# A two-stage mixture-of-experts kernel: the hand-written order of work where its two stages meet is planned anew

## The reference, cut to what matters

```python
x = x + xattn(layernorm(x), token_ids, ctx)   # 4 experts, chosen by token id
x = x + ffn(layernorm(x), router_w, wg, wu, wd)  # 8 experts, chosen by argmax of the logits
# xattn, expert e:  y = (silu(h @ ctx[e].T) * (h @ ctx[e].T)) @ ctx[e].T
# ffn, expert e (bitlinear: weights to -1, 0, 1 times a mean; activations to int8 by row):
#   y = bitlinear(relu(bitlinear(h, wg[e]))**2 * bitlinear(h, wu[e]), wd[e])
```

## Time and profile before

| | |
|---|---|
| median of 3 runs | 247.35 us (246.73 to 247.69) |
| the profiled execution | 247.17 us |
| its span, first to last instruction | 245.3 us |
| mean granted TensorE clock | 0.989 |
| PE, DVE, ACT, POOL busy | 218.7, 209.0, 197.7, 160.4 us |

### The profile page before, as it was taken

The page is one execution under the profiler, slowest core; times in us unless marked ns, Lnnn a source line. Parts: engine busy times, 40 slices in busy tenths (PEclk is TensorE's granted clock), DMA queues, the critical chain, the costliest instruction groups (busy, mean ns, idle before and its releaser), DMA issues.

```text
span 245.3 us, 6263 instructions
## 1 busy us (share of the span) xinstructions
PE 218.7 (89%) x1622; PEld 170.4 (69%) x1629; DVE 209.0 (85%) x696; ACT 197.7 (81%) x297; POOL 160.4 (65%) x324
## 2 busy tenths in 40 slices
PE   2398999999999999999999999987789999899970
PEld 2245688889899999999999998976334544343430
DVE  5969999977969899899988999979799998888771
ACT  2757799877768889998999979896678998788860
POOL 5262667756637598888987887553734878557762
PEclk9999999999999999999999999999979999999998
DMA  5999999996985266679565786335328899994120
GB/s 199 426 319 383 413 421 385 402 378 187 392 302 174 81 263 218 254 261 339 166 245 212 251 252 220 95 122 178 97 50 241 289 293 366 379 387 190 65 108 13
DMA packets 14273, 61.44 MB, mean 250 GB/s; under 512 B 2654, under 2 KB 2654, under 8 KB 9632
## 3 DMA queue, kind: packets, MB, share of 16 engines
q1 hardware_dynamic: 9600, 47.60, 53.6%
q0 software_dynamic: 4640, 13.44, 15.6%
HBM read 43.88 MB, written 12.70 MB: 231 GB/s over the span
## 4 chain that ended last, share of the span: by engine, by line
PE 68%; DVE 14%; DMA 7%; issue 6%; ACT 3%; POOL 1%; DVEq 0%; ACTq 0%; POOLq 0%
PE banks L1834 35%; PE banks L2014 15%; PE banks L1817 7%; DMA ternary<-weight_chunks 4%; PE banks L2016 4%; DMA x<-x_rows,gather 2%; PE banks L2003 2%; PE banks L1979 2%; PE banks L1859 2%; POOL out_rows L778 1%; DVE stats L1249 1%; DVE row L1305 1%; PE banks L1887 1%; DVE ternary L1108 1%; DVE p L1285 1%
## 5 line engine op out<-in xcount | busy, mean ns | idle before, releaser
L833 ACT ACTIVATE ternary<-staged 128x2048 bf16<-128x2048 f32 x20 | 38.1, 1906 | 1.8 <-DMA staged<-weight_chunks 1.8
L2014 PE MATMUL banks<-ternary,qT 128*128 x126 | 34.6, 394 | 3.3 <-ACT qT L922 1.6
L839 ACT ACTIVATE ternary<-staged,w_scale 128x1536 int16<-128x1536 f32 (+1 forms) x20 | 34.4, 1724 | 2.9 <-DVE w_scale L1202 2.9
L692 POOL DMA_INDIRECT x_rows<-row,store_at x19 | 22.3, 1172 | 9.3 <-POOL store_at L684 6.9
L1834 PE MATMUL banks<-ctx_hi,pT_hi 128*128 x132 | 23.0, 313 | 1.7 <-DVE row L1305 1.1
L594 POOL DMA_INDIRECT x<-x_rows,gather x16 | 18.3, 1145 | 9.2 <-DVE gather L1120 6.3
L647 POOL TENSOR_TENSOR row<-ln,half_powers 128x2 f32<-128x2 f32 x19 | 14.1, 744 | 14.9 <-DVE squares L1320 14.9
L2014 PEld LDWEIGHTS banks<-ternary,qT 128*128 128x128 bf16 x128 | 12.4, 101 | 16.4 <-issue 8.5
L1834 PE MATMUL banks<-ctx_hi,hT_hi 128*128 x132 | 22.8, 312 | 0.0
L1834 PE MATMUL banks<-ctx_lo,hT_hi 128*128 x132 | 21.2, 300 | 0.2 <-DVE ctx_lo L1149 0.2
L1834 PE MATMUL banks<-ctx_hi,pT_lo 128*128 x132 | 21.3, 301 | 0.0
(11 more groups left out here) (284 smaller groups left out, 641.0 us busy)
## 6 DMA issues: line engine op xcount, KB each, us to landing
staged<-weight_chunks SPq DMA_DIRECT2D x20, 1024.0 KB
twin<-ternary SPq DMA_DIRECT2D x4, 1536.0 KB
ternary<-ctx_chunks SPq DMA_DIRECT2D x4, 1024.0 KB, 7.9
ternary<-weight_chunks SPq DMA_DIRECT2D x4, 1024.0 KB, 12.3
ternary<-ctx_rows SPq DMA_DIRECT2D x4, 1024.0 KB, 11.0
late_rows<-x_rows SPq DMA_DIRECT2D x11, 260.0 KB, 3.0
x_rows<-filler SPq DMA_DIRECT2D x1, 2080.0 KB
staged<-x_rows SPq DMA_DIRECT2D x5, 260.0 KB, 3.5
```

Of the source, the lines that this page charges most:

```text
L692: pool.indirect_dma_start(x1_rows, bass.IndirectOffsetOnAxis(ap=store_at[b % ROWS][:, :], axis=0), row[b % ROWS][:, :], None, bounds_check ...
L833: nc.scalar.activation(ternary[:, m * K * D:(m + 1) * K * D], staged_of(i), ACT.Abs, accum_out=abs_sum[:, 2 * i:2 * i + 1]).then_inc(abs_r ...
L839: nc.scalar.activation(ternary[:, m * K * D + first:(m + 1) * K * D].bitcast(I16), staged_of(i)[:, first:], ACT.Copy, scale=w_scale[:, m:m ...
L2014: last = pe.matmul(ps[:, :], rows, ternary[:, columns], start=(k == 0), stop=(k == K - 1))
```

## The change

- EARLY becomes 6 and EARLY_AFTER 15: six slots are planned from the counts of blocks 0 to 15, and 14 are left for later. GROUPS, LATE and the places follow.
- The last second product (block 18) writes the half banks 4 and 5, those of the first products, and waits for `kept_ready` in place of the residual of block 17. The gate products of stage 2 start in bank 3 instead of 4.
- The sum of matrix 20 moves into first_product(18), ahead of its third pass; that of matrix 21 stays ahead of the third pass of second_product(18), and its result goes to bank 7. transpose_q(0) goes to the same place.
- The loops of DVE, ACT and PE end a tick sooner (at t = 17), and the rest is written out in a new order; the nine steps of `early_slots` now begin at the end of tick 17 and are strewn over what follows.
- down_product(1) waits until `late_slots` has read the counts.

The diff, cut to its core (`next(early)` and `next(factors)` are one step each):

```diff
-EARLY, EARLY_AFTER = 5, 14
+EARLY, EARLY_AFTER = 6, 15
+        def second_banks(b):
+            return (4, 5) if b == B1 - 1 else (2, 3)
+        def mean_ps(i, n=1):
+            return bank[7][:, 300:300 + n] if i == len(ORDER) - 1 else bank[6][:, 64 + 2 * i:64 + 2 * i + n]
-        g_ps, u_ps = [bank[4], bank[3]], [bank[1], bank[2]]
+        g_ps, u_ps = [bank[3], bank[4]], [bank[1], bank[2]]
 # ACT, behind the loop
+            evict_pT(B1 - 2)
+            scale_piece(*EXTRA_SCALES[B1 - 1])
+            scale_part(B1 - 1 + ABOVE)
+            silu(B1 - 1)
+            square(B1 - 3)
             evict_pT(B1 - 1)
             sum_abs(B1 + ABOVE)
             square(B1 - 2)
+            evict_tT(0)
             scale_part(B1 + ABOVE)
-            evict_tT(0)
+            evict_tT(1)
             square(B1 - 1)
-            evict_tT(1)
             relu_of(0)
+            evict_tT(2)
             square_of(0)
-            evict_tT(2)
             relu_of(1)
+            evict_tT(3)
             square_of(1)
             copy_by_slot(0)
             quantise_prod(0)
-            evict_tT(3)
 # DVE, end of tick 17 and behind the loop
+                if t == B1 - 2:
+                    next(early)
+                if t > 2:
                     cut(t + ABOVE - 1)
+            next(early)
+            cut(B1 - 2 + ABOVE)
+            next(early)
+            sum_logits(B1 - 3)
+            residual(B1 - 3)
+            next(early)
+            top_logits(B1 - 3)
+            negative_mean(B1 - 3)
+            next(early)
+            choice(B1 - 3)
+            mean_of(B1 - 1 + ABOVE)
+            scale_of(B1 - 1 + ABOVE)
+            scale_part(B1 - 1 + ABOVE)
+            one_hot(B1 - 3)
+            pT_rest(B1 - 2)
+            extra_cut(EXTRA_CUT[B1])
+            next(early)
+            gate(B1 - 1)
+            keep_logits(B1 - 1)
+            next(early)
             cut(B1 - 1 + ABOVE)
+            row_index(B1 - 3)
+            next(early)
+            largest(B1 - 3)
+            next(early)
+            pT_rest(B1 - 1)
+            sum_logits(B1 - 2)
+            residual(B1 - 2)
+            negative_mean(B1 - 2)
+            quantise(0)
+            top_logits(B1 - 2)
+            choice(B1 - 2)
             mean_of(B1 + ABOVE)
             scale_of(B1 + ABOVE)
             scale_part(B1 + ABOVE)
+            one_hot(B1 - 2)
+            quantise(1)
             sum_logits(B1 - 1)
             residual(B1 - 1)
+            negative_mean(B1 - 1)
+            row_index(B1 - 2)
+            largest(B1 - 2)
             top_logits(B1 - 1)
             choice(B1 - 1)
+            quantise(2)
             one_hot(B1 - 1)
+            next(factors)
+            largest(B1 - 1)
+            next(factors)
             row_index(B1 - 1)
+            next(factors)
             product_of(0)
+            next(factors)
+            next(factors)
+            quantise(3)
             largest_product(0)
             cut(B1 + ABOVE)
             first_factors()
             product_scale(0)
-            quantise(3)
             late = late_slots()
 # PE
+        # first_product(18), ahead of pass n == 2: sum_mean(B1 - 1 + ABOVE)
+        # second_product(17), n == 1: rank(B1 - 3); n == 2: transpose_p(B1 - 1)
+        # second_product(18), n == 2: sum_mean(B1 + ABOVE), transpose_q(0)
+                if b == B1 - 1:
+                    pe.wait_ge(kept_ready, B1 - FOLD)
+            transpose_p(B1 - 2)
+            first_product(B1 - 1)
+            second_product(B1 - 2)
+            count_in(B1 - 3)
+            load_ffn_expert(0)
             second_product(B1 - 1)
-            transpose_q(0)
-            load_ffn_expert(0)
+            rank(B1 - 2)
             gate_product(0)
-            rank(B1 - 1)
             transpose_q(1)
             up_product(0)
             load_ffn_expert(1)
-            count_in(B1 - 1)
+            count_in(B1 - 2)
             gate_product(1)
+            rank(B1 - 1)
             transpose_q(2)
             up_product(1)
             load_ffn_expert(2)
+            count_in(B1 - 1)
             spread_means(0)
             gate_product(2)
             transpose_q(3)
```

More of the change, by code:

```diff
@@ L320, in y_of @@
         def y_of(b):
-            return y_ps if b < FOLD else banks[:, 2 * D + D // 2:3 * D + D // 2]
+            first = second_banks(b)[0] * D + D // 2
+            return y_ps if b < FOLD else banks[:, first:first + D]
         def chosen(t):
             return [b for b in (t - 3,) if b < FOLD] + [b for b in (t - 2,) if b >= FOLD]
-        counts_ps, mean_ps, logits_ps = bank[6][:, 0:E2], bank[6], bank[7]
+        counts_ps, logits_ps = bank[6][:, 0:E2], bank[7]
+        def mean_ps(i, n=1):
+            return bank[7][:, 300:300 + n] if i == len(ORDER) - 1 else bank[6][:, 64 + 2 * i:64 + 2 * i + n]
         tT_ps = bank[0][:, 0:D // 4].bitcast(BF16)
-        g_ps, u_ps = [bank[4], bank[3]], [bank[1], bank[2]]
+        g_ps, u_ps = [bank[3], bank[4]], [bank[1], bank[2]]
         rT_ps, d_ps = bank[7][:, 0:D // 4].bitcast(BF16), [bank[5], bank[6]]
@@ L990, in _ @@
             sum_abs(3)
-            for t in range(2, TICKS):
+            for t in range(2, B1 - 1):
                 evict_pT(t - 1)
@@ L1653, in _ @@
             early, factors = early_slots(), mean_products()
-            for t in range(2, TICKS):
-                interlude = early if t == EARLY_AFTER + 3 else iter(())
+            for t in range(2, B1 - 1):
                 first, *second = chosen(t)
@@ L1844, in columns_of @@
                 if second:
-                    return [(bank[2][:, half:], LEFT, half), (bank[3][:, 0:half + E2], LEFT + half, half + E2)]
+                    lower, upper = second_banks(b)
+                    return [(bank[lower][:, half:], LEFT, half), (bank[upper][:, 0:half + E2], LEFT + half, half + E2)]
                 return [(bank[4][:, half - E2:], 0, half + E2), (bank[5][:, 0:half], LEFT + half, half)]
@@ L1886, in sum_mean @@
                     pe.wait_ge(w_mean_ready, i)
-                pe.matmul(mean_ps[:, 64 + 2 * i:64 + 2 * i + n], ones[:, :], abs_sum[:, 2 * i:2 * i + n],
-                          start=False, stop=True, skip_group_check=True).then_inc(mean_ready, 1)
+                if i == len(ORDER) - 2:
+                    pe.wait_ge(counts_read, 1)
+                pe.matmul(mean_ps(i, n), ones[:, :], abs_sum[:, 2 * i:2 * i + n], start=(i == len(ORDER) - 1),
+                          stop=True, skip_group_check=True).then_inc(mean_ready, 1)
             def transpose_h(b):
@@ L1939, in ahead @@
                     def ahead(n):
+                        if n == 1:
+                            rank(B1 - 3)
                         if n == 2:
@@ L1946, in ahead @@
                     def ahead(n):
-                        if n == 1:
-                            rank(B1 - 2)
                         if n == 2:
-                            count_in(B1 - 2)
                             sum_mean(B1 + ABOVE)
+                            transpose_q(0)
                             pe.wait_ge(pT_lo_ready, B1)
-                if b >= 1:
+                if b == B1 - 1:
+                    pe.wait_ge(kept_ready, B1 - FOLD)
+                elif b >= 1:
                     pe.wait_ge(x1_ready, b)
@@ L2125, in down_product @@
                     pe.wait_ge(relu_ready, B2 - 1)
-                elif b > 1:
+                elif b == 1:
+                    pe.wait_ge(counts_read, 2)
+                else:
                     pe.wait_ge(out_ready, b - 1)
@@ L2154, in _ @@
             second_product(0)
-            for t in range(2, B1):
+            for t in range(2, B1 - 1):
                 transpose_p(t - 1)
```

56 lines of the change are left out of this document (15 added, 41 removed).

## The result

| | before | changed |
|---|---|---|
| median of 11 runs each, side by side | 246.89 us | 248.71 us |
| ratio, 95% interval | | 1.0068 (1.0047 to 1.0088) |
| profiled execution, its span | 247.17, 245.3 us | 248.56, 246.7 us |
| mean granted TensorE clock | 0.989 | 0.981 |
| PE, DVE, ACT, POOL busy | 218.7, 209.0, 197.7, 160.4 | 217.8, 208.3, 197.6, 160.9 |

The changed kernel is slower by 0.7%, some 1.7 us. I had forecast 248.3 us, with "within 0.5%" as the likeliest of the three outcomes; it came out just beyond that bound. Executions far above the others of their kernel (more than 1.5% above its fastest) are left out of every ratio in this document; each ratio is against executions of the kernel before that were timed with that kernel.

What follows compares the result with a forecast made beforehand. PE was taken to bound both stages, DVE's quantise(4) the meeting; -0.15 (DVE) + 1.1 (clock) + 0 (six slots) = +0.95, giving 248.3 us from the median of 247.35; 8 in 10 range 245.8 to 249.8.

Steps and rivals of the forecast that it cites:

- Transpose_q(4): Where the stages meet: its start on PE sets the meeting's cost, and DVE's quantise(4) sets it; forecast at 182.35, before 182.50.
- Tick 17: End of stage 1: PE runs 0.8 us sooner, DVE wins nothing; residual(16) at 158.4, before 158.53.
- The new wait before second_product(17): PE stands 1.8 us for pT_rest(17), behind about 1.0 us more DVE work; second_product(17) at 161.6, before 160.75.
- The removed wait: Before second_product(18) on PE: the 1.07 us wait goes, 0.75 of it already spent one product earlier; start at 165.1, before 165.41.
- Gate_product(0): First gate product of stage 2, called the largest gain on PE: at 168.5 instead of 170.6, 2.1 us sooner.
- rival 4: Longer wait before second_product(17), gate_product(0) only 1.5 sooner, transpose_q(4) late by 0.3: 248.8 us with the clock; chance 0.07.
- Copy_by_slot(0): ACT's copy, behind the eviction of slot 3, holds DVE 1.2 us; first_factors at 177.35, before 176.69.
- The step behind it: On DVE from first_factors: L1583 0.52 us behind, then 3.9 to quantise(4) at 181.75, before 181.90; DVE gains 0.15 us.
- The clock: Longer PE gaps let the low clock reach over transpose_q(4) at 182.35, costing 1.1 us, range 0 to 2.6.
- rival 3: Low clock granted before 182.35 holds for two stretches, 5.2 us of it behind that point: 249.8 us; chance 0.15.
- The six slots: The sixth early slot costs 0 us, hidden behind PE, with 0.2 to either side.
- Rival 1: DVE not held by copy_by_slot, so quantise(4) 1.4 us sooner and the low clock ends before the work: 245.95 us; chance 0.25.

Runs made afterwards that it cites:

- e2: Changed kernel with ACT's evict_tT(3) moved behind square_of(1) and copy_by_slot(0); ratio 1.0008 to the kernel before.
- e4: Changed kernel with the last second product back in half banks 2 and 3, waiting for block 17's residual, gate products from bank 4; ratio 1.0126 to before.
- e1: Changed kernel with 25 matmuls that nobody reads in PE's three gaps (6, 10 and 9); ratio 0.9996 to the kernel before.
- e5: Changed kernel with five early slots instead of six (fifteen late ones); ratio 1.0083 to the kernel before.
- e6: Changed kernel with evict_tT(3) behind copy_by_slot(0) on ACT and 6, 4 and 9 unread matmuls in PE's gaps; ratio 0.9975 to the kernel before.
- e11: Changed kernel with unread matmuls in PE's first two gaps only (6 and 10), the last left open; ratio 1.0012 to the kernel before.
- e3: Kernel before with 4 unread matmuls ahead of spread_means(0) and 5 ahead of transpose_q(3); ratio 0.9996 to the kernel before.
- e8: Changed kernel with the edits of e6 and e7 together, and silu(18) ahead of scale_part(20) on ACT; ratio 0.9980 to the kernel before.
- e7: Changed kernel with one_hot(16) and pT_rest(17) on DVE back ahead of mean_of, scale_of and scale_part of matrix 20; ratio 1.0079 to the kernel before.

## Why the prediction was right, and where it was off

Starts are given behind residual(15), since that takes the scatter of stage 1 out; my own anchors stood on the trace of before, with residual(15) at 150.60.

- **Transpose_q(4) is the point, and DVE sets it**: right. e2 and e4 moved quantise(4) by -1.1 and +1.6 us, and transpose_q(4) went with it, -1.1 and +1.6.
- **Tick 17 gains nothing on DVE**: right. residual(16) comes 8.05 us behind residual(15), before 7.93; forecast 158.4 - 150.6 = 7.8.
- **The new wait before second_product(17)**: right in kind, 1.42 us where I had 1.8; second_product(17) 10.94 behind, forecast 11.0.
- **The removed wait**: right; second_product(18) 14.54 behind residual(15), forecast 14.5.
- **Gate_product(0)**: forecast 17.9, measured about 18.5 (its first record is missing, 18.68 for the second). The term left out is rank(17), which stands ahead of it on PE and waited 0.31 us for one_hot(17) from DVE. It is 1.5 us sooner than before where I had 2.1, as in rival 4, but product_of(0) did not come later for it.
- **Product_of(0)**: 22.90, forecast 22.85; before 23.27.
- **Copy_by_slot(0)**: right; first_factors at 26.84, forecast 26.75, behind an idle time of 1.21 for which I had 1.2. e2 shows that this idle time is all that the new place of evict_tT(3) costs, 1.1 us.
- **The step behind it was the wrong one on DVE.** From first_factors to L1583 (L1599 here) I had "0.52 behind"; it is 177.39 - 176.51 = 0.88. The "3.9" from there to quantise(4) is right, 181.27 - 177.39 = 3.88. What failed is that I took the idle time of 0.25 behind L1583 off, as if it went with quantise(3). A pause did not go: 0.46 of idle time now stands ahead of L1599 instead, in e2_copy_first as well, and the whole way from first_factors to quantise(4), 4.76, is what it was before without quantise(3) (5.21 - 0.46 = 4.75). What the pause is stays open. With first_factors 0.09 later, DVE does not gain 0.15 us but loses 0.3 (quantise(4) 31.60 against 31.30).
- **The clock: the mechanism was right, the size was off.** I took 1.1 us of a range of 0 to 2.6; it is 2.0 (64.8 against 62.8), and e1 shows that it is the clock. The term that was too small is the overlap: I took a low stretch of 3.4 us, as before, with about 2.2 of it behind transpose_q(4); it lasted 6.8 us, twice as long, with 4.2 behind it, and half of 4.2 is 2.1. The double length I had as rival 3 with 0.15. (I also wrote that the low level of before lasted to "shortly before 182.50"; it ended at 181.7, and the 3.4 us that I reckoned with are right.) So the outcome lies between the forecast and that rival: -0.15 + 1.1 became +0.3 + 2.0.
- **The six slots at 0**: right, within the 1 us or so that e5 can tell.
- **Rival 1** (DVE not held by copy_by_slot) would have been a good kernel, not the changed one: e6 is that kernel, with a full clock, and brings transpose_q(4) 0.85 us ahead of before, not 1.4.

The chances followed the forecast too closely: both errors, 0.45 us on DVE (31.15 forecast, 31.60 measured) and 0.9 on the clock, went the same way, and together they carried it over the bound of 0.5%. That 248.71 lies only 0.4 us from 248.3 is in part luck: the forecast change was 0.95 us and the measured one some 1.7, but I started from 247.35 and the kernel before, timed side by side, had 246.89.

## What to carry to other kernels

Before an order is rewritten to free PE, find the last start that another engine sets and follow that engine's list to it: here PE was 1.5 us sooner at gate_product(0) and 2.5 us sooner at transpose_q(3), and first_factors on DVE was still 0.75 us later than before, since one eviction had been put ahead of a 0.17 us copy that DVE needed. An idle gap of PE is not free even where it is off the path: if it ends where PE becomes the bound, a low clock can reach over and cost half of what lies behind that point (2.0 us for 4.2 here). Cheap matmuls that nobody reads, placed in the gap, both measured that and cured it here.

## What the runs showed that was not expected

- With some of the gaps filled, the mean clock is a matter of the single execution: the same kernel gave 246.4 us at a mean clock of 0.994 or more and 248.2 at 0.990 or less (e11).
- Fillers in the last gap alone, or in the two before it alone, each went with a mean clock of 0.994 or more in a part of the executions; with all three gaps filled, eleven of twelve had 0.991 or more (e1).
- With the clock full in the kernel before, the time gained ahead of transpose_q(4) turned into 1.96 us of waiting for the same quantise(4) (e3).
- A later scale_part on ACT (0.9 us) left so little margin that one load, which took 4.9 us to land instead of 2.8, made DVE wait 1.32 us; with the same delay and a load of 2.8 us there was no wait (e8, e7).
